# Computing 36 of 256 expert units inside the attention stage of a sandwich layer, on eight cores

## The reference

```python
x = x + layernorm(attn(layernorm(x)))
x = x + layernorm(ffn(layernorm(x)))
```

## Time and profile before

| | us |
|---|---|
| runs of the kernel before | 7069.66, 7072.94, 7167.7 (median 7072.94) |
| the profiled execution | 7070.67, span 7069.1 on its slowest core |
| spans of the 8 cores | 7064.6 to 7069.1 |
| mean granted PE clock of each core | 0.902 to 0.903 of full |
| PE busy | 5713.2 (81%) |
| DVE busy | 3209.9 (45%) |
| ACT busy | 794.6 (11%) |
| POOL busy | 164.9 (2%) |

### The profile page before, as it was taken

One profiled execution on the slowest core, in us unless ns is written; L12 is line 12 of the kernel. 1 busy time (PEld: TensorE's weight loads), 2 busy tenths in 40 slices (PEclk: granted clock), 3 DMA queues, 4 the chain that ended last, 5 costly groups with the idle time before them and its releaser, 6 DMA issues.

```text
span 7069.1 us, 71337 instructions; the slowest of 8 cores (7064.6 to 7069.1 us)
## 1 busy us (share of the span) xinstructions
PE 5713.2 (81%) x26240; PEld 2568.3 (36%) x26240; DVE 3209.9 (45%) x4436; ACT 794.6 (11%) x1347; POOL 164.9 (2%) x202
## 2 busy tenths in 40 slices
PE   2222222218999999999999999999999999999992
PEld 0001011103444444444444444444444444444441
DVE  4666666663434343434343434344343434343437
ACT  0000111101111111111111111111111111111111
POOL 0000000000000000000000000000000000000000
PEclk7555666659999999999999999999999999999996
DMA  3000000003222232222223322222232222223312
GB/s 71 0 24 0 24 0 12 0 12 54 36 36 36 40 47 40 36 36 36 36 36 45 45 36 36 36 36 36 40 46 41 36 36 36 36 36 44 46 19 95
DMA packets 173421, 247.85 MB, mean 35 GB/s; under 512 B 3616, under 2 KB 134688, under 8 KB 171552
## 3 DMA queue, kind: packets, MB, share of 16 engines
q0 software_dynamic: 169056, 209.74, 20.6%
q1 hardware_dynamic: 4032, 33.56, 1.4%
HBM read 436.22 MB, written 16.78 MB: 64 GB/s over the span
## 4 chain that ended last, share of the span: by engine, by line
PE 80%; DVE 14%; issue 3%; ACT 1%; DMA 1%; another core or an unknown queue 0%; DVEq 0%; ACTq 0%; POOL 0%; POOLq 0%
PE ps_g L507 25%; PE ps_u L512 25%; PE ps_d L538 25%; PE ps_mm L260 3%; DVE prod L332 2%; DVE prod L290 2%; DVE prod L328 2%; DVE prod L286 2%; PE ps_att L364 1%; DVE scr L144 1%; PE ps_mm L256 0%; DMA wd_b<-wd 0%; DVE stats L145 0%; DVEq L73 0%
## 5 line engine op out<-in xcount | busy, mean ns | idle before, releaser
L522 DVE TENSOR_TENSOR hbuf<-silb,ps_u 128x512 bf16<-128x512 bf16 x1024 | 704.3, 688 | 2890.8 <-PE ps_u L512 2890.8
L507 PE MATMUL ps_g<-ln2T,wg_b 128*128 128x512 bf16 x8192 | 1936.9, 379 | 37.1 <-DMA wd_b<-wd 37.1
L512 PE MATMUL ps_u<-ln2T,wu_b 128*128 128x512 bf16 x8192 | 1936.2, 379 | 0.0
L538 PE MATMUL ps_d<-hbuf,wd_b 128*128 128x512 bf16 x8192 | 1809.7, 379 | 0.0
L548 DVE TENSOR_TENSOR acc<-ps_d,acc 128x512 f32<-128x512 f32 x2016 | 1393.6, 692 | 330.4 <-PE ps_d L538 303.1
L507 PEld LDWEIGHTS ps_g<-ln2T,wg_b 128*128 128x128 bf16 x8192 | 801.7, 98 | 1004.8 <-issue 39.0
L512 PEld LDWEIGHTS ps_u<-ln2T,wu_b 128*128 128x128 bf16 x8192 | 802.0, 98 | 967.3 <-issue 1.8
L538 PEld LDWEIGHTS ps_d<-hbuf,wd_b 128*128 128x128 bf16 x8192 | 801.6, 98 | 966.5
L518 ACT ACTIVATE silb<-ps_g 128x512 bf16<-128x512 f32 x1024 | 611.4, 597 | 4676.0 <-PE ps_g L507 4675.9
L207 PE MATMUL ps_tr<-ident,ctxt 128*128 128x128 bf16 x128 | 16.2, 306 | 850.3 <-DVE ctxt L340 850.3
L207 PEld LDWEIGHTS ps_tr<-ident,ctxt 128*128 128x128 bf16 x128 | 12.4, 138 | 857.7 <-issue 857.7
(11 more groups left out here) (80 smaller groups left out, 1059.3 us busy)
## 6 DMA issues: line engine op xcount, KB each, us to landing
wg_b<-wg POOLq DMA_DIRECT2D x64, 1024.0 KB, 12.3
wu_b<-wu POOLq DMA_DIRECT2D x64, 1024.0 KB, 19.3
wd_b<-wd POOLq DMA_DIRECT2D x64, 1024.0 KB, 23.7
xf<-x SPq DMA_DIRECT2D x4, 2048.0 KB, 11.0
xspill<-xf SPq DMA_DIRECT2D x4, 2048.0 KB, 7.1
xrel<-xspill SPq DMA_DIRECT2D x4, 2048.0 KB, 10.4
out<-outb SPq DMA_DIRECT2D x16, 512.0 KB, 2.6
wqkv_sb<-wqkv POOLq DMA_DIRECT2D x1, 6144.0 KB, 52.6
```

The lines of the kernel that those rows point to most:

```text
L507: gt = op('t', lambda t, par=par, kh=kh, kd=kd, bk=bk, toks=toks: t.matmul(ps_g[:, bk], wg_b[:, par, kd, kh * 128:(kh + 1) * 128], ln2T[:, ...
L512: ut = op('t', lambda t, par=par, kh=kh, kd=kd, bk=bk, toks=toks: t.matmul(ps_u[:, bk], wu_b[:, par, kd, kh * 128:(kh + 1) * 128], ln2T[:, ...
L522: mul_tok[c] = op('v', lambda v, kh=kh, bk=bk, c=c, q=q: v.tensor_tensor(hbuf[:, q % 2, kh], silb[:, c % 2], ps_u[:, bk], ALU.mult), MUL)
L538: dt_ = op('t', lambda t, par=par, m=m, mi=mi, kh=kh, q=q: t.matmul(ps_d[:, mi], wd_b[:, par, kh, m * 128:(m + 1) * 128], hbuf[:, q % 2, k ...
```

## The change

The first 36 of the 64 weight groups are no longer computed for the first 512 tokens in stage B. These 36 units are computed in stage A, from the fifth tile on: after S5(t) for t = 4 to 15 the program appends three weight groups (`ov_gp`), so 12 x 3 = 36. Since SBUF and PSUM are already full in stage A, each weight group is done as two chunks of 256 hidden columns, with buffers of their own:

- `wg_o`, `wu_o`, `wd_o`: two sets; each chunk has three casting DMAs of half the size, issued by POOL, that wait for the last matmul of the chunk before the previous one.
- `og`, `ou`: one PSUM bank each. The gate matmuls of a block wait for the Silu and the product of the block before.
- `od`: two PSUM banks. Each chunk makes 8 output blocks of only 2 matmuls each, and DVE adds each into `acc_j0` in SBUF. An output block waits for the add of the one two before it.

To make room, stage A loses its second halves: `ln1`, `ln1T`, `prod`, `ctxt`, `ctxT`, `ln2tok`, `scr`, `ps_tr`, `ps_mm` and `ps_att` are single, `tmpl` is replaced by `scr`, and `xf` holds four tiles, each loaded and spilled by itself. The waits `- 2` become `- 1`.

After the last tile `acc_j0` (2 MB) is written to HBM (`accspill`) by SP, the first weight loads of stage B wait for that, and it is read back into `acc[:, :, 0:512]`. In stage B the list `qs` holds the 220 remaining units; a weight group below 36 has three units, the others four. Those weight groups are still loaded again in stage B for the other three token groups.

```diff
@@ stage A buffers
-    xf = Sa("xf", [128, 2, 4, D], F32)
+    xf = Sa("xf", [128, 4, D], F32)
...
-    prod = Sa("prod", [128, 2, 4096], BF16)
+    prod = Sa("prod", [128, 4096], BF16)
...
-    ps_tr = Pa("ps_tr", [128, 2, 8, 128], BF16)
-    ps_mm = Pa("ps_mm", [128, 2, 512], F32)
-    ps_att = Pa("ps_att", [128, 2, 2, 512], F32)
+    ps_tr = Pa("ps_tr", [128, 8, 128], BF16)
+    ps_mm = Pa("ps_mm", [128, 512], F32)
+    ps_att = Pa("ps_att", [128, 2, 512], F32)
+    acc_j0 = Sa("acc_j0", [128, 8, 512], F32)
+    wg_o = Sa("wg_o", [128, 2, 8, 256], BF16)
+    wu_o = Sa("wu_o", [128, 2, 8, 256], BF16)
+    wd_o = Sa("wd_o", [128, 2, 2, D], BF16)
+    hb_o = Sa("hb_o", [128, 2, 2, 512], BF16)
+    sb_o = Sa("sb_o", [128, 2, 512], BF16)
+    og = Pa("og", [128, 512], F32)
+    ou = Pa("ou", [128, 512], F32)
+    od = Pa("od", [128, 2, 512], F32)
@@ S3
-            if n_qg[0] - 2 in tok_qkv_evac:
-                QE.wt('t', tok_qkv_evac[n_qg[0] - 2])
+            if n_qg[0] - 1 in tok_qkv_evac:
+                QE.wt('t', tok_qkv_evac[n_qg[0] - 1])
@@ S4, both halves
-            if gg - 2 in tok_prod:
-                VV.wt('v', tok_prod[gg - 2])
+            if gg - 1 in tok_prod:
+                VV.wt('v', tok_prod[gg - 1])
@@ new, called after S5
+    def ov_gp(gp):
+        e, gi2 = divmod(gp, NG)
+        for half in range(2):
+            ch = ov_ch[0]; ov_ch[0] += 1
+            par = ch % 2
+            if ch - 2 in ov_mmd:
+                OD.wt('g', ov_mmd[ch - 2])
...
+            WO[par].wt('t', wo_cnt[par])
...
+            for kh in range(2):
+                c = ov_c[0]; ov_c[0] += 1
+                if c - 1 in ov_sil:
+                    OS.wt('t', ov_sil[c - 1])
+                    OM.wt('t', ov_mul[c - 1])
...
+            OM.wt('t', ov_mul[ov_c[0] - 1])
+            for m in range(8):
+                d = ov_dn[0]; ov_dn[0] += 1
+                sl = d % 2
+                if d - 2 in ov_acc:
+                    OA.wt('t', ov_acc[d - 2])
...
+                OD.wt('v', dt_)
...
+                    ov_acc[d] = op('v', lambda v, m=m, sl=sl: v.tensor_add(
+                        acc_j0[:, m], od[:, sl], acc_j0[:, m]), OA)
@@ loop of stage A
         S4(t_i)
         S5(t_i)
+        if t_i >= 4:
+            for _ in range(3):
+                if ov_next[0] < OV_GPS:
+                    ov_gp(ov_next[0])
+                    ov_next[0] += 1
@@ before stage B
+    if OV_GPS > 0:
+        OA.wt('y')
+        op('y', lambda e: e.dma_start(accsp_d, acc_j0[:]), ASP, 16)
@@ stage B
+    qs = [q for q in range(NQ) if not (q % 4 == 0 and q // 4 < OV_GPS)]
```

More of the change, by code:

```diff
@@ L264, in S3 @@
             tok_qkv_evac[n_qg[0]] = op(
-                's', lambda s, n=n, b=b, p2=p2: s.activation(
-                    qkv[:, p2, n * 512:(n + 1) * 512], ps_mm[:, b], AF.Copy), QE)
+                's', lambda s, n=n, p2=p2: s.activation(
+                    qkv[:, p2, n * 512:(n + 1) * 512], ps_mm[:], AF.Copy), QE)
             n_qg[0] += 1
@@ L347, in S5 @@
     def S5(t_i):
-        p2 = t_i % 2
         VV.wt('t', tok_hm_done[t_i])
-        if t_i >= 2:
-            MM.wt('v', tok_wout_mm[t_i - 2])
-        trt2, ev2 = transpose_batch(lambda k, p2=p2: ctxt[:, p2, k * 128:(k + 1) * 128], ctxT[:, p2])
+        if t_i >= 1:
+            MM.wt('s', tok_wout_mm[t_i - 1])
+        trt2, ev2 = transpose_batch(lambda k: ctxt[:, k * 128:(k + 1) * 128], ctxT[:])
         tok_ctx_tr[t_i] = trt2
@@ L398, in S7 @@
         VE.wt('t', w_ln2)
-        _, ev = transpose_batch(lambda k, p2=p2: ln2tok[:, p2, k * 128:(k + 1) * 128],
+        _, ev = transpose_batch(lambda k: ln2tok[:, k * 128:(k + 1) * 128],
                                 ln2T[:, :, t_i * 128:(t_i + 1) * 128])
         tok_ln2_ev[t_i] = ev
[L402 to L408, removed]
+        VE.wt('y', w_ln2)
@@ new lines, in S7 @@
+        op('y', lambda e, t_i=t_i: e.dma_start(xsp_d[:, t_i], xf[:, t_i % 4]), SP, 16)
+        if t_i + 4 < nt_lim:
+            SP.wt('y')
+            op('y', lambda e, t_i=t_i: e.dma_start(xf[:, t_i % 4], x_d[:, t_i + 4]),
+               XL4[t_i % 4], 16)
+    OV_GPS = 36 if (mode != 'A' and nt_lim == NT) else 0
+    WO = [Ch("WOa"), Ch("WOb")]
+    OG = Ch("OG"); OU = Ch("OU"); OD = Ch("OD")
+    OS = Ch("OS")
+    OM = Ch("OM"); OA = Ch("OA")
+    ASP = Ch("ASP"); AIR = Ch("AIR")
+    wo_cnt = [0, 0]
@@ L410, in build @@
+    ov_next = [0]
     S1(0)
@@ L493, in emit_P1 @@
         toks = slice(jj * 512, (jj + 1) * 512)
-        if jj == 0:
+        if jj == (0 if gp >= OV_GPS else 1):
             emit_weights(gp)
@@ L502, in emit_P1 @@
                 MUL.wt('t', mul_tok[c - 2])
-            if kh == 0 and q - 2 in mmd_q:
-                MMD.wt('v', mmd_q[q - 2])
+            if kh == 0 and idx - 2 in mmd_i:
+                MMD.wt('v', mmd_i[idx - 2])
             gt = None
@@ L532, in emit_P2 @@
                 m = half * 4 + mi
-                pk = (q, 0, mi) if half == 1 else (q - 1, 1, mi)
+                pk = (idx, 0, mi) if half == 1 else (idx - 1, 1, mi)
                 if pk in accw_tok:
@@ L537, in emit_P2 @@
                 for kh in range(4):
-                    dt_ = op('t', lambda t, par=par, m=m, mi=mi, kh=kh, q=q: t.matmul(
-                        ps_d[:, mi], wd_b[:, par, kh, m * 128:(m + 1) * 128], hbuf[:, q % 2, kh],
+                    dt_ = op('t', lambda t, par=par, m=m, mi=mi, kh=kh, idx=idx: t.matmul(
+                        ps_d[:, mi], wd_b[:, par, kh, m * 128:(m + 1) * 128], hbuf[:, idx % 2, kh],
                         start=(kh == 0), stop=(kh == 3)), MMD if kh == 3 else None)
                 MMD.wt('v', dt_)
+                if first_p2[0] and half == 0 and mi == 0:
+                    SP.wt('v', spill_done)
+                    first_p2[0] = False
+                if jj == 0 and not air_waited[0]:
+                    AIR.wt('v', 16)
+                    air_waited[0] = True
                 if gp == 0:
-                    if q == 0 and half == 0 and mi == 0:
-                        SP.wt('v', spill_done)
                     tok = op('v', lambda v, m=m, mi=mi, toks=toks: v.tensor_copy(
```

238 lines of the change are left out of this document (144 added, 94 removed).

## The result

| | us |
|---|---|
| runs of the changed kernel | 7571 to 7584, and two of 7658 and 7676 |
| runs of the kernel before that agree with each other | 7068 to 7073 |
| ratio, 95% interval | 1.0745 [1.0664, 1.0827] |
| the profiled execution | 7571.2, span 7569.3 on its slowest core |
| forecast | 7840, range 7600 to 8100 |

The kernel is 7% slower, not 11%. The runs of 7658 and 7676 raise this ratio; the other four are 1.071 to 1.073 of the kernel before and lie 16 to 29 us under the range.

A forecast was written before the change was run, and what follows sets the result against it. It took the expert stage as bound by PE and the attention stage by PE and DVE taking turns. 7069.1 - 746 + 1362 (chunks) + 146 (single buffers) + 8 (start) = 7839, stated as 7840 us, range 7600 to 8100.

The forecast's parts named there:

- Removed from the expert stage: Expert stage, bound by PE alone: 36 units at 20.72 us each leave it, saving 746 us.
- The order: Attention stage: chunks start only after S4, nothing runs beside them, so 12 tiles each grow by their whole six-chunk stretch.
- A chunk without waiting for weights: Attention stage: one chunk takes 15.8 us, 9.5 for gate and up, 6.3 for eight output blocks.
- The weights: Chunk loads in the attention stage: 17.2 us of flow, priced by run; PE waits 5.4, 1.4, 4.0 and 1.4 a tile.
- lead of 3.7 us: Chunk loads: time from a load's issue until its data starts to flow, 3.7 us, ahead of the 17.2 us of flow.
- low bound of 10.9: Chunk loads: flow time if half the bytes cost half the full 21.8 us, 10.9 us.
- weights are no wait: Rival for the chunk loads: half a load costs half the time, stretch 97.1 us, total 7642; chance 0.17.
- Single buffers: All 16 attention tiles: `ps_mm`, `ps_tr` and `prod` being single cost 9.1 us a tile, 146 us.
- Start of stage B: First weight loads of the expert stage wait for the 2 MB spill of `acc_j0`: 8 us, between 0 and 15.
- The rule on runs of 512 B: Chunk loads: transfers from 512 B on go at line rate, which would give 7642 us; the forecast set it aside.
- Half clock in the stretch: Rival: PE's clock stays at half in the chunks, stretch 151.7 us, total 8297; chance 0.13, in part or in all.
- Not slower by overlap: Rival: chunks run in PE's idle time beside S4, 41.4 us a tile, total 6974, 1.3% faster; chance 0.02.

The follow-up runs named there:

- e4_inter: Changed kernel with 24 groups instead of 36 in the attention stage, two a tile, their instructions placed within S4 instead of after S5: 7054.6 us.
- e3_split: Kernel before the change, each gate and up load of the expert stage cut into two loads of 256 columns: span 7074.7 us.
- e11_late: Changed kernel with each chunk's weight loads issued one chunk later, when the chunk just before it ends: 8482 to 8520 us on cores 0 to 3.
- e2_noload: Changed kernel without the chunks' weight loads after the first two chunks: span 7561.8 us.
- e10_bank: Changed kernel with a second PSUM bank for S3, the first half of `ps_att`, and nothing else: span 7481.9 us.
- e7_more: Changed kernel's 36 groups placed within S4 and S6, down products in one piece, DVE allowed to wait up to 0.9 us: 6909 to 6917 us on cores 0 to 3.

## Why the forecast was right and wrong

**Removed from the expert stage**: 746 forecast, 746 measured. A stage that is full of matmuls loses what its matmuls took.

**The order**: right. The wait for `ctxt` went from 850 to 867 us, no chunk stands in it, and a tile grew by its whole stretch. e4_inter shows it as the cause: moved into S4, the same chunks cost less than half.

**A chunk without waiting for weights**: 15.8 forecast, 15.0 measured. Gate and up were right (9.4 against 9.5). The output part takes 5.6 us, not 6.3: DVE does its adds two by two with 0.25 us between the pairs, so two blocks take 1.54 and not 1.71. Which hop of the round was priced too long the rows don't tell. 0.8 x 72 = 58 us.

**The weights**: this is the step that failed. The forecast said "I take 7.3 + 7.3 + 2.6 = 17.2 us, the end that the rows lie near to". It took the difference between the gate load and the down load in the earlier trace rows, 8.3 and 5.2 us, for a price by run. e3_split shows no such price: twice as many runs of half the size have landed after 24.9 us, not 38. A chunk's loads have landed 12.8 us after their first issue, and e11_late shows PE 12 to 13 us of waiting when nothing covers them, in the place of 21.2. With the forecast's own lead of 3.7 us, 12.8 leaves 9.1 us of flow, less than even its low bound of 10.9. So the rival "weights are no wait" was the case, which had 0.17; e2_noload confirms it, where leaving the loads out gains 7.5 us. Its time, 7642, is still 71 us above the profiled execution, since it kept the forecast's chunk, single buffers and start. Waits and the clock behind them, priced at 16 us a tile, were next to none: 194 us. With the chunk's 58 that is 252; the term missed by 249 (1362 against 1113), and the few us between lie at the edges of the stretch. (The forecast's 111, 0.8 and 1.5 us make 113.3 a tile, not 113.5.)

**Single buffers**: 146 forecast, 129 measured. The gap of `ps_mm` is 0.84 and not 1.2 us (S3 groups start 3.04 us apart, before 2.15). Against that, the gaps did delay the full clock in most tiles (e10_bank), which the forecast had only in its upper bound; the two errors partly cancel.

**Start of stage B**: 8 forecast, 4 measured.

**The rule on runs of 512 B** (the Trainium skill, DMA: Bandwidth & Descriptors, Specifications), which the forecast set aside, is in accord with e3_split, which has runs of 512 B: 24.9 against 25.5 us. The rows had shown two loads of different shape, which is not a test of run size.

**Half clock in the stretch**: it was 1.00 in the stretch of six chunks, in spite of gaps of 1.0 us after each block and 0.35 in the output part. The warning of the Trainium skill that was cited beside this rival doesn't come true in the stretch. In S3 something like it does: there PE comes out of an idle time at half clock, and with gaps of 0.84 us between groups it mostly reaches full clock a group later than without them (e10_bank). Where PE waited 12 us (e11_late) it did start at half.

**Not slower by overlap**: the price of this rival, 41.4 us a tile for 60 DVE instructions and 6974 in all, was a fair one for two groups a tile: e4_inter needs 29 for 40. For three it was too low: e7_more, with only 36 instructions a tile, needs some 38, since DVE then waits for the chunks' matmuls too.

## What to carry to other kernels

Idle time of an engine is no room for more work as long as its instructions wait, in order, for the other engine's whole step; new work has to be put between the instructions of that step, on both engines. Then its price is at least the busy time that it adds to the engine that sets the pace (e4_inter, 29 us for 27.6; e7_more, 38 for 25), so first cut that (adds over four matmuls instead of two), and take banks back that a stage doesn't use. And when a wait is priced from two rows that differ in more than one thing, keep both bounds alive: here the difference between them, 265 us, was a third of the forecast loss.

## What was not expected

Loads of the same size land sooner in the changed kernel's expert stage. In the kernel before, the 8 cores issue `wg_b` within 4.6 us of each other, and the third load lands 21.7 to 24.8 us after its issue. In the changed kernel the issues are spread over 17 us, and on core 6 it reads

```profile
wd_b<-wd POOLq DMA_DIRECT2D x39, 1024.0 KB, 17.1
```

with 17.1 to 21.8 on the eight cores. That the cores slow each other when they load together fits this, and would also explain why gate and up took longer than down in the earlier trace rows. e3_split fits it too: there the cores issue within 9.9 us of each other, and `wd_b` lands 16.6 to 24.0 us after its issue on the eight; but that run also cut the loads. It is only argued: no run changed the spacing of the cores by itself.
